# A one-core transformer block (feed-forward, attention, feed-forward): second feed-forward stage prepared in the output stage, new order of loads at the join, packed fp32r adapters in the first feed-forward stage

## The reference

```
x = x + 0.5 * ffn(layernorm(x))
x = x + attention(layernorm(x))        # 32 heads, low-rank queries and keys, causal softmax
x = x + 0.5 * ffn(layernorm(x))

def ffn(x, weight, bias, lora_A, lora_B, starts):      # the same weights both times
    y = x @ weight.T + bias
    seg = searchsorted(starts, arange(B), side='right') - 1
    adapter = clip(seg - 1, 0, 2)                      # one of 3 adapters of rank 16, by sequence
    lo = (x @ lora_A[adapter].T) @ lora_B[adapter].T
    return y + where(seg > 0, lo, 0)
```

## Time and profile before

| | before |
|---|---|
| median of the 3 runs shown | 1924.73 us (lowest 1918.6) |
| the profiled execution | 1922.07 us, span 1919.9 us |
| first feed-forward stage | 2 to about 243 us |
| latents, attention | about 243 to 1340 us |
| output stage | to about 1703 us |
| second feed-forward stage | 1706.6 us to the end |

### The profile page before, as it was taken

The page is one execution under the profiler, slowest core; times in us unless marked ns, Lnnn a source line. Parts: engine busy times, 40 slices in busy tenths (PEclk is TensorE's granted clock), DMA queues, the critical chain, the costliest instruction groups (busy, mean ns, idle before and its releaser), DMA issues. The chain is left out here.

```text
span 1919.9 us, 44288 instructions
## 1 busy us (share of the span) xinstructions
PE 1809.1 (94%) x15472; PEld 1420.9 (74%) x15472; DVE 1233.0 (64%) x2653; ACT 998.3 (52%) x2135; POOL 870.5 (45%) x641
## 2 busy tenths in 40 slices
PE   6999959899999999999999999997799999969999
PEld 3778859877777777777777777775688888857887
DVE  5565348788898888988889898887422111125553
ACT  2211047788887888878788787885311000012210
POOL 2232111377777878778787777873000000014321
PEclk9999979999999999999999999999899999979999
DMA  6542152311212212121121212213643332225321
GB/s 221 179 154 98 66 164 94 83 59 52 85 60 75 65 53 79 56 84 51 67 79 56 80 50 72 72 65 127 204 132 96 103 107 87 66 110 175 121 90 64
DMA packets 111698, 182.48 MB, mean 95 GB/s; under 512 B 27473, under 2 KB 64465, under 8 KB 109585
## 3 DMA queue, kind: packets, MB, share of 16 engines
q1 hardware_dynamic: 111632, 181.61, 29.5%
HBM read 122.06 MB, written 59.51 MB: 95 GB/s over the span
## 5 line engine op out<-in xcount | busy, mean ns | idle before, releaser
L1194 PE MATMUL psS<-keyT,q 128*128 128x512 f32 (+2 forms) x2304 | 472.0, 350 | 23.9 <-POOL q L570 14.1
L1194 PEld LDWEIGHTS psS<-keyT,q 128*128 128x128 f32 x2304 | 380.2, 189 | 118.1 <-DVE negmax L1311 42.4
L1261 ACT ACTIVATE prob<-prob,negmax 128x640 f32<-128x640 f32 (+7 forms) x512 | 392.0, 767 | 78.2 <-DVE negmax L1311 75.6
L1321 DVE STREAM_TRANSPOSE pT<-prob 128x640 f32<-128x640 f32 (+7 forms) x512 | 379.9, 762 | 66.5 <-PE psV L1211 61.7
L1311 DVE CUSTOM_DVE_ANT_0 prob<-psS,mask 128x640 f32<-128x640 f32 (+7 forms) x512 | 371.7, 742 | 19.7 <-PE psS L1194 6.2
L421 PE MATMUL f_psy<-f_weff,f_xT 128*128 128x512 f32 x1344 | 313.5, 392 | 0.0
L1007 PE MATMUL psS<-o_w,o_o 128*128 128x512 f32 x1344 | 304.8, 389 | 0.0
L1007 PEld LDWEIGHTS psS<-o_w,o_o 128*128 128x128 f32 x1344 | 252.3, 188 | 52.4
L421 PEld LDWEIGHTS f_psy<-f_weff,f_xT 128*128 128x128 f32 x1344 | 250.8, 188 | 53.7 <-issue 1.7
L1211 PE MATMUL psV<-pT,val 32*64 32x512 f32 (+3 forms) x8192 | 265.8, 408 | 7.2 <-DVE pT L1321 6.2
L1211 PEld LDWEIGHTS psV<-pT,val 32*64 32x64 f32 x8192 | 169.2, 132 | 111.2 <-issue 67.3
(11 more groups left out here) (113 smaller groups left out, 1914.9 us busy)
## 6 DMA issues: line engine op xcount, KB each, us to landing
wo<-in_wo SPq DMA_DIRECT2D x16, 1024.0 KB, 5.8
pT<-row_scales SPq DMA_DIRECT2D x128, 128.0 KB, 2.9
oT<-pT SPq DMA_DIRECT2D x64, 256.0 KB, 2.5
o_in<-oT SPq DMA_DIRECT2D x32, 512.0 KB, 5.3
f_xt<-in_x SPq DMA_DIRECT2D x16, 512.0 KB, 4.3
f_w_in<-in_w SPq DMA_DIRECT2D x16, 512.0 KB, 6.2
w_sum<-f_w_in SPq DMA_DIRECT2D x16, 512.0 KB, 5.3
x<-f_xo SPq DMA_DIRECT2D x16, 512.0 KB, 3.0
```

Source lines behind the costliest of these rows:

```text
L1194: ins = nc.tensor.matmul(psS[:, slot, start + x0:start + x1], q[:, e, a, t * P:(t + 1) * P], k.keyT[:, m, b * S + x0:b * S + x1], start=(i ...
L1261: nc.scalar.activation(row, row, ACT.Exp, bias=negmax[:, n % 8:n % 8 + 1], scale=-1.0, accum_out=rowsum[:, column(n, s):column(n, s) + 1]) ...
L1321: nc.vector.transpose(pT[:, n % 2, t, 0:width], prob[:, n % RING, 0:width]).then_inc(turned, 1)
```

## The change

**Adapters, first feed-forward stage.** A and B are packed into 48 of 64 rows (3 adapters of rank 16) and loaded twice, into partitions 0 to 63 and 64 to 127, in four DMAs; `wanted` comes by a DMA too. ScalarE makes `b_hi` and the high part of A; GpSimd sets `b_lo` (zero in the upper rows, B minus `b_hi` in the lower); VectorE takes A minus its high part in the upper rows; then A is gated. The outer product of a piece is four fp32r matmuls with 128 rows instead of two fp32 matmuls with 96.

**Output stage.** `behind` is 8 instead of 4; the loads of the last round stand in another order; VectorE and ScalarE split weights 0 to 7 ahead of the last values' eviction, where it was 0 to 3.

**Second feed-forward stage.** A new object `Early` owns the first four slots of `w_in`, `xt` and `xn` of that stage and lays them over memory that the output stage has freed. In the output stage SP loads pieces 0 to 3 once all pairs are split, and tiles 0 and 1 once tile 14 is multiplied; VectorE and ScalarE normalise both ahead of tile 15's sums. SP no longer waits for the last stores at the end of the stage: SP (before the bias load), ScalarE (before piece 1) and GpSimd (before the first bias add) of the next stage wait for them (`vacated`).

```
@@ ffn_phase, sync
+                a_d, b_d, starts_d, wanted_d = adapters
+                sp.dma_start(wanted[:], wanted_d[:, :]).then_inc(starts_in, 16)
+                for rows in (slice(0, PACKED), slice(PACKED, P)):
+                    sp.dma_start(lora_b[rows, :], b_d[:, :]).then_inc(b_in, 16)
+                for rows in (slice(0, PACKED), slice(PACKED, P)):
+                    sp.dma_start(lora_a[rows, :], a_d[:, :]).then_inc(a_in, 16)
+            vacated(sp)
             sp.dma_start(bias_half[:], ...)
@@ ffn_phase, gpsimd
+                pool.wait_ge(b_split, 1)
+                nc.gpsimd.tensor_tensor(b_lo[0:PACKED, :], lora_b[0:PACKED, :], b_hi[0:PACKED, :].bitcast(F32),
+                                        ALU.subtract).then_inc(b_rest, 1)
             pieces_low([0])
             pool.wait_ge(halved, 1)
+            vacated(pool)
@@ ffn_phase, scalar
             def pieces_hi(pieces):
+                    if early is not None and i == 1:
+                        vacated(act)
+                act.wait_ge(b_in, 32)
+                nc.scalar.activation(b_hi[:], lora_b, ACT.Copy).then_inc(b_split, 1)
+                act.wait_ge(a_in, 32)
+                nc.scalar.activation(gated[:, 0, :], lora_a, ACT.Copy).then_inc(a_split, 1)
@@ ffn_phase, tensor, outer_products
                 for half in range(2):
-                    ins = nc.tensor.matmul(ps_w[:, half, :], gated[...], lora_b[...], start=True, stop=True)
+                    nc.tensor.matmul(ps_w[:, half, :], gated[:, i // DT, x], b_hi[:, y], start=True, stop=False)
+                    ins = nc.tensor.matmul(ps_w[:, half, :], gated[:, i // DT, x], b_lo[:, y], start=False, stop=True)
@@ ffn_phase, vector
+            def adapters_lo():
+                dve.wait_ge(a_split, 1)
+                nc.vector.tensor_tensor(lora_a[PACKED:P, :], lora_a[PACKED:P, :],
+                                        gated[PACKED:P, 0, :].bitcast(F32), ALU.subtract).then_inc(a_rest, 1)
@@ Early
+    def load_weights(self, sp):
+        for i in range(SLOTS):
+            sp.dma_start(self.w_in[:, i, :], self.sum_d[i * P:(i + 1) * P, :]).then_inc(self.w_loaded[i], 16)
+    def load_tokens(self, sp, src_d):
+        for n in range(2):
+            sp.wait_ge(self.x_stored[n], 16)
+            sp.dma_start(self.front.xt[:, n, :], src_d[n * P:(n + 1) * P, :]).then_inc(self.front.x_in[n], 16)
@@ Output.sync_steps
+        sp.wait_ge(self.w_lo, PAIRS)
+        self.early.load_weights(sp)
+                if not later(n, NT) and n == NT - 1:
+                    sp.wait_ge(self.product, 2 * NT - 2)
+                    self.early.load_tokens(sp, self.dst_d)
-        for j in range(2):
-            sp.wait_ge(self.y_stored[j], 16 * NT // 2)
@@ Output.vector_steps (and the square roots in scalar_steps)
+            if not later(n, NT) and n == NT - 1:
+                for m in range(2):
+                    self.early.front.stats_of(nc, dve, m, m, loads_of(m, m))
+                    self.early.front.normalise(nc, dve, m, m)
@@ Output.tensor_steps
-        behind = 4
+        behind = 8
@@ attention_phase, sync
-                    if r.last and s == 1 and (job, n) == ("X", 0):
+                    if r.last and s == 0 and (job, n) == ("X", 1):
                         ...
                         output.load_weights(sp, range(SLOTS))
-                    if r.last and s == 1 and job == "Z":
+                    if r.last and s == 0 and (job, n) == ("Y", 1):
+                        sp.wait_ge(w_done, units)
                         sp.wait_ge(o_stored[0], 16 * (units - 1))
                         output.load_outputs(sp, 0)
-                    if r.last and s == 1 and (job, n) == ("X", 1):
-                        output.load_weights(sp, range(SLOTS, 2 * SLOTS))
+                    if r.last and s == 1 and job == "Z":
                         sp.wait_ge(output.o_lo, 2)
                         output.load_outputs(sp, 1)
+                        output.load_weights(sp, range(SLOTS, 2 * SLOTS))
@@ attention_phase, scalar and vector
                             output.weights_hi(nc, act, range(SLOTS))
+                            act.wait_ge(turned, TILES * units)
+                            output.weights_hi(nc, act, range(SLOTS, 2 * SLOTS))
-                            output.weights_lo(nc, dve, range(SLOTS))
+                            output.weights_lo(nc, dve, range(2 * SLOTS))
```

More of the change, by code:

```diff
@@ L33 @@
 STARTS = 4
-GATED = 32 * ADAPTERS
+PACKED = 64
 QT = S // P
@@ L222, in ffn_phase @@
             ps_w = c.ps(tag + "ps_w", [P, 2, BANK])
[L223 to L231 removed]
+            lora_a, lora_b = xo[:, 0, :], xo[:, 1, :]
+            b_lo = c.sb("lora_b_lo", [P, D], F32R)
+            b_hi = c.sb("lora_b_hi", [P, D], F32R)
+            gated = c.sb("gated", [P, B, D], F32R)
+            starts = c.sb("starts", [P, STARTS], I32)
+            startf = c.sb("startf", [P, STARTS])
+            hit = c.sb("hit", [P, B, STARTS])
+            count = c.sb("count", [P, B])
+            wanted = c.sb("wanted", [P, 1])
+            chosen = c.sb("chosen", [P, B])
             starts_in, a_in, b_in = c.sem("starts_in"), c.sem("lora_a_in"), c.sem("lora_b_in")
[L233 removed]
+            chain, gate, cleared = c.sem("chain"), c.sem("gate"), c.sem("lora_cleared")
+            a_split, b_split, a_rest, b_rest = c.sem("lora_a_hi"), c.sem("lora_b_hi"), c.sem("lora_a_lo"), c.sem("lora_b_lo")
         bias_in, halved = c.sem(tag + "bias_in"), c.sem(tag + "halved")
[L235 removed]
         w_stored = [c.sem(tag + f"w_stored{j}") for j in range(SLOTS)]
@@ L248, in piece_ready, with vacated @@
                 eng.wait_ge(summed, i + 1)
+        def vacated(eng):
+            if early is not None:
+                for j in range(2):
+                    eng.wait_ge(early.x_stored[j], 16 * NT // 2)
         def low(engine, i):
@@ L319, in add_bias @@
                     pool.wait_ge(stored[j], (n - j) * 8)
+                elif w_d is not None:
+                    pool.wait_ge(gate, B)
                 nc.gpsimd.tensor_tensor(xo[:, j, :], f.xt[:, j, :], bias_half[:], ALU.add).then_inc(with_bias, 1)
@@ L901, in __init__ @@
         self.product, self.result = c.sem("o_product"), c.sem("o_result")
-        self.y_stored = [c.sem(f"o_y_stored{j}") for j in range(2)]
+        self.y_stored = early.x_stored
+        self.early, self.eps = early, eps
     def half_of(self, h):
@@ L1295, in _ @@
             rounds(act, body)
-            act.wait_ge(turned, TILES * units)
-            output.weights_hi(nc, act, range(SLOTS, 14))
+            output.weights_hi(nc, act, range(2 * SLOTS, 14))
             for ch in range(2):
@@ L1366, in _ @@
             rounds(dve, body)
-            output.weights_lo(nc, dve, range(SLOTS, PAIRS))
+            output.weights_lo(nc, dve, range(2 * SLOTS, PAIRS))
             output.vector_steps(nc, dve)
@@ L1411, in output_steps, with macaron_block @@
     steady(eng, step, NT, 1, 1, start=0)
-def macaron_block(nc, x, wa, lnw, wn, wpe, wv, wo, cos, sin, cosT, sinT, w, bias, lora_a, lora_b, starts, out):
+def macaron_block(nc, x, wa, lnw, wn, wpe, wv, wo, cos, sin, cosT, sinT, w, bias, lora_a, lora_b, starts, wanted, out):
     x1_d = nc.dram_tensor("x1", (T, D), F32).ap()
@@ L1430, in macaron_block @@
         constants_phase(nc, k)
-        ffn_phase(nc, "f1_", k, x, x1_d, bias, sum_d, w, (lora_a, lora_b, starts))
+        ffn_phase(nc, "f1_", k, x, x1_d, bias, sum_d, w, (lora_a, lora_b, starts, wanted))
+        k.early = Early(c, sum_d)
         with ExitStack() as inner:
```

132 lines of the change are left out of this document (77 added, 55 removed).

## The result

The changed kernel takes 1908.0 us (median of 5 runs, 1906.9 to 1909.8) against 1924.5 us before; the ratio is 0.9923 with a 95% interval of 0.9912 to 0.9934, which is 13 to 17 us less. I forecast 1901, so the change brought some 15 us where 21.2 were summed up. One early run of the kernel before, of 5604.57 us, is a disturbed one and no part of any comparison.

The account below looks back on a forecast made before the run. TensorE, busy for 94% of the span, was taken as the bound. Gains of 6.0 (stage 1), 3.0 (output join) and 12.2 (second-stage preparation), 21.2 us off the profiled 1922.07, gave 1901; own range 1896 to 1904, wide range 1890 to 1910.

Parts of the forecast that it names:

- Outer products: Stage 1, TensorE: four fp32r matmuls take 0.91 us a piece against 1.72; pieces 11 to 15 gain 4.05 us.
- Start of stage 1: Adapter preparation ahead of the first outer product: a longer chain loses 1.6 us, bounds 0 and 3.
- the chain of a_lo: Stage 1 start: a_lo on VectorE waits beside GpSimd's b_lo, ends about 16.15; gating to 16.95, first sum at 18.8.
- The loads of 64 rows: Adapter loads at stage 1's start: about half rate, A's rows near 14.4, making the start's loss 2.0 instead of 1.6.
- Fill of stage 1: Pieces 2 to 10, ahead of tile 2: pieces 6 to 10 gain 3.5 us, bounds 0 and 7.3.
- Stage 1, the step that failed: First feed-forward stage in all: 4.05 + 3.5 - 1.6 = 6.0 us gained, bounds 3 and 9.
- Output join: Join of attention and output stage: earlier loads and eight pairs behind gain 3.0 us; pair 8 starts at 1360.3.
- the output join gives nothing: Rival, chance 0.17: loads from weight 8 on still stand behind the last stores; 1904, or 1906 with 2 lost.
- Preparation of the second stage: Join of output and second feed-forward stage: tiles 0 and 1 prepared beside the last tile's matmuls gain 12.2 us.
- the wide 1890 to 1910: Whole kernel: range holding all but late preparation, the half clock in stage 1's fill and the author's mistakes.

Follow-up runs that it names:

- layout_moved: The changed kernel with 64 unused bytes per partition ahead of weff in stage 1, nothing else touched: 1902.2 us, ratio 0.9893.
- join_undone: The changed kernel with the output join of the kernel before (4 pairs behind, loads and splits in old places): 1909.4 us, ratio 0.9929.

## Why the prediction was right and wrong

- **Outer products, right.** 0.91 us a piece instead of 1.72 was forecast; a tile with one takes 0.92 more than one without (13.00 against 12.08), and it takes 13.79 with the old adapters in the same layout. Five tiles at 0.79 are 3.9 us, forecast 4.05.
- **Start of stage 1, wrong by 1.6 in our favour.** The step that failed is the chain of a_lo. GpSimd's b_lo was put at 12.5 to 14.9; it ran at 10.79 to 13.14, since statistics and root came 1.2 us earlier (VectorE's first copy of the adapter starts had waited until 7.50 before, until 6.30 now). So a_lo started at 12.44 and not 13.5, took 1.79 us and not 2.68, and the first outer product started at 15.17, not 16.95. The sum of piece 0 started at 17.33, as before (17.36). One reading of mine was wrong on the way, without harm to the sum: the row at 13.79 (3.46 us, four matmuls) is one piece and not two, since the trace records an fp32 matmul of the adapters twice; the next piece is the row at 18.64.
- **The loads of 64 rows.** They took 4.5 and 5.7 us from issue to landing (256 KB each), where 6.5 stood in the earlier trace rows. ScalarE took up A's rows at 11.35. The estimate that I made from the Trainium skill ("SBUF — State Buffer", section "Door 1: The DMA port swizzle") had them at 14.4; this case's rows decide against that estimate, but not against the page's halved rate, with which the trace agrees: 214 to 231 GB/s were moved at 5 to 11 us, while these loads ran, and 416 behind them, with loads of 128 rows. No run here measured one such load alone.

```profile
f_xo<-in_lora_b SPq DMA_DIRECT2D x2, 256.0 KB, 4.5
f_xo<-in_lora_a SPq DMA_DIRECT2D x2, 256.0 KB, 5.7
```

```profile
5.00:7.00 2.00, 0.00 (x0) 0.00 (x0) 0.59 (x4) 0.00 (x0) 0.00 (x0) 1.00 0.88 214
...
11.00:13.00 2.00, 1.83 (x8) 1.43 (x8) 0.56 (x1) 1.06 (x1) 2.00 (x1) 1.00 1.04 416
```

- **Fill of stage 1, a bit too high.** Tile 2 was to start 1.9 us earlier (3.5 less 1.6). It starts at 68.78 against 71.22 with the old adapters in the same layout: 2.4. Since nothing was lost at the start, the pieces brought 2.4 where I took 3.5.
- **Stage 1, the step that failed.** The sum was built on "one fp32r matmul of 128x512 costs 10.90 / 48 = 0.227 us", taken from the second stage before. I held that for a property of the instruction. It is one of the instruction and of where its operands lie, and the diff moves the tiles: the line that allocates weff stands below xT in it. In stage 1 each took 6.6 ns more, 5.1 us over 768 matmuls. The adapters alone brought the 6.0 that I took (5.0 to 6.9); the stage as a whole brought 1.3 in the profiles.
- **Output join, mechanism right, size wrong: 0.7, not 3.0.** I named what is late next, the loads of weights 8 to 15 behind the last stores, and had TensorE start pair 8 at 1360.3. It came at 1361.94. GpSimd scaled the last rows in 3.58 us, not 2.6, weight 8 left SP at 1355.28, not 1354.4, and took 4.2 us, not 3.5, to ScalarE. The rest is the clock behind a wait of 10.8 us. 144 matmuls took 35.5 us; I had 34.5, with the slow start costing 1.8. The rival "the output join gives nothing" (0.17) was nearly true, by its mechanism too: the loads from weight 8 on behind the last stores.
- **Preparation of the second stage, right: 12.1 to 12.2** forecast against 12.1 between three profiles and eight, and each row of the way as described. Here the mechanism held, and not only the number.
- **The total.** Forecast 6.0 + 3.0 + 12.2 = 21.2. By the runs: adapters some 6, join 0.7, preparation 12.1, layout -5.1: 13.7, within the 13 to 17 that the times give. The median of 1908 lies outside the 1896 to 1904 of the forecast itself and inside the wide 1890 to 1910. That it stayed inside is in part luck: the layout was in none of the cases for which the range was made. Within stage 1 the start (1.6 better) and the fill (1.1 worse) nearly cancelled. With the layout put right (layout_moved) the time is 20.6 us below the kernel before, by its ratio (17.7 to 23.5). The profiled execution of after lost 0.8 between stage 1 and the scores (they start at 364.91 against 365.35), and 1.4 in the first 30 score matmuls (7.78 us against 6.40); join_undone had the same stage 1 and started its scores at 362.75, so that is scatter and no effect of the change.

## What to carry to other kernels

When a diff reorders allocations, work out the distances between the operands of the matmuls as you work out instructions: here the one line that moved a tile cost 5.1 us, nearly what a rewrite of the adapters won, and 64 unused bytes gave it back. Check it by the cheapest row there is, the duration of a group of matmuls that the diff does not touch. And when you forecast what is late next, as I did with the loads behind the stores, that is already the next edit: moving four loads past two stores in a queue was worth 7 to 9 us at that place and 5.0 in the time, far more than the new order of pairs and loads around it, at 0.7 to 0.8.

## What was not expected of the hardware

A matmul in fp32r of 512 columns takes 0.227 us back to back when stationary and moving operand lie a multiple of 256 bytes apart in a partition, and 5.5 to 7 ns more when the moving one lies 32, 96, 128 or 192 bytes past that, in the loops of the feed-forward stages (48 in a row: 11.14 to 11.19 against 11.40 to 11.46 us). In the output stage distances of 64 (even tiles) and 192 (odd tiles) cost 3.9 ns a shifted matmul in the mean (two tiles of 96: 43.89 against 43.52 us). With 384 columns in the latent stage nothing could be seen, and in the scores at most 1.5 us in all. Why, no run here shows.
